# A graph network's edges as two streams on 128 partitions: scans of 64 by 1024 become scans of 128 by 512

## The reference, cut to what matters

```python
def prop(h):                                           # layer 0: Chebyshev, twice
    return segment_sum(w[:, None] * h[src], dst, num_segments=n)
# layer 0 goes on with a softmax over the edges of a node (segment_max, exp, segment_sum), 4 heads,
o = segment_sum(xh[s2] * alpha[:, :, None], d2, num_segments=n)
# layer 1: messages mlp(relu(norm(x[src]))) * et, summed per dst;   layer 2: relu(... @ W + b), summed per dst
# layer 3: hh = [x_dst, x_src - x_dst] @ W.T + b per edge, batch norm over the edges, leaky relu, mean per dst
```

## Time and profile before

| | |
|---|---|
| median of 3 runs | 5640.05 us (5634.35 to 5642.95) |
| span of the profiled execution | 5641.0 us |
| busy: PE, DVE, ACT, POOL | 3732.6, 4168.8, 2361.1, 3788.1 us |

### The profile page before, as it was taken

How to read it: one execution, slowest core, us unless ns; L and a number is a source line. 1 busy time by engine, 2 the same in 40 slices (tenths; PEclk the granted TensorE clock), 3 DMA queues, 4 the chain that set the end, 5 groups by cost and what they waited for, 6 DMA issues and landing times. The chain is left out here.

```text
span 5641.0 us, 69641 instructions
## 1 busy us (share of the span) xinstructions
PE 3732.6 (66%) x15267; PEld 1851.4 (33%) x15267; DVE 4168.8 (74%) x6266; ACT 2361.1 (42%) x4957; POOL 3788.1 (67%) x3734
## 2 busy tenths in 40 slices
PE   8997788847776999677727876777555546552110
PEld 3443555533332333244414442333222212221000
DVE  8876789957774555788868988999655559996442
ACT  0000678833331222466618973343222247772221
POOL 7776766767775777577724337666377767774777
PEclk9998899977876555788869998899766568885555
DMA  5533987744442222455524433333244423332221
GB/s 59 77 53 56 153 203 226 234 136 107 107 106 55 61 63 61 141 182 171 181 64 129 137 117 76 82 83 82 79 130 131 131 69 76 76 73 65 68 72 51
DMA packets 538641, 595.34 MB, mean 106 GB/s; under 512 B 300576, under 2 KB 315046, under 8 KB 536923
## 3 DMA queue, kind: packets, MB, share of 16 engines
q1 hardware_dynamic: 319004, 473.91, 28.7%
q0 software_dynamic: 115712, 91.82, 9.1%
q10 hardware_dynamic: 103840, 28.71, 4.2%
HBM read 354.69 MB, written 303.31 MB: 117 GB/s over the span
## 5 line engine op out<-in xcount | busy, mean ns | idle before, releaser
L1135 POOL DMA_INDIRECT l_got<-d_x,l_near x1176 | 1157.6, 984 | 557.5 <-issue 354.6
L1135 POOL DMA_INDIRECT p_got<-d_h,p_near x392 | 440.2, 1123 | 155.8 <-issue 118.9
L848 PE MATMUL ps<-hot_lo,hot_w 128*128 128x512 bf16 x2352 | 510.0, 380 | 13.4 <-DVE hot_lo L785 13.4
L1135 POOL DMA_INDIRECT p_got<-d_sums,p_near x392 | 401.4, 1024 | 151.7 <-issue 149.3
L2457 POOL DMA_INDIRECT out<-fi_res,fi_near x392 | 381.0, 972 | 181.1 <-issue 118.2
L726 POOL DMA_INDIRECT d_pos<-place,near x392 | 400.2, 1021 | 125.2 <-issue 119.1
L1135 POOL DMA_INDIRECT p_got<-d_ext,p_near x392 | 382.2, 975 | 132.4 <-issue 117.1
L1143 POOL DMA_INDIRECT ln_xd<-d_xt,idsE x304 | 286.9, 944 | 136.8 <-issue 96.9
L2131 PE MATMUL ps<-l_hid,w2n 128*64 128x512 f32 x392 | 234.8, 756 | 162.2 <-DVE l_sums L1308 155.7
L412 PE MATMUL ps<-ident,fi_sums 64*128 64x64 f32 x392 | 53.1, 314 | 424.8 <-DVE fi_sums L1308 424.8
L848 PEld LDWEIGHTS ps<-hot_lo,hot_w 128*128 128x128 bf16 x2352 | 230.6, 98 | 293.2 <-issue 17.3
(11 more groups left out here) (391 smaller groups left out, 10871.3 us busy)
## 6 DMA issues: line engine op xcount, KB each, us to landing
l_xd<-d_x SPq DMA_DIRECT2D x147, 256.0 KB
d_ext<-ln_ext SPq DMA_DIRECT2D x98, 264.0 KB
d_xt<-in_x_wide ACTq DMA_DIRECT2D x49, 520.0 KB
ln_x<-in_x SPq DMA_DIRECT2D x98, 256.0 KB
d_h<-ln_hb SPq DMA_DIRECT2D x98, 256.0 KB, 2.9
d_x<-ln_x SPq DMA_DIRECT2D x98, 256.0 KB
lb_x<-d_x SPq DMA_DIRECT2D x49, 512.0 KB
d_x<-lb_x SPq DMA_DIRECT2D x49, 512.0 KB
```

The costliest lines, as they stand in the source:

```text
L848: last = nc.tensor.matmul(bank(h), hot_w[:, r, k], hot_lo[:, r, 512 * h:512 * h + 512], start=False, stop=False)
L1135: nc.gpsimd.indirect_dma_start(out=out[:, q], out_offset=None, in_=source, in_offset=bass.IndirectOffsetOnAxis(ap=ids[:, q:q + 1], axis=0) ...
```

## The change

The padded edges are cut in the middle into two streams of 25,088 (STREAM). The first runs upward from edge 0; the second is turned round and runs downward from the last edge, so that they meet in the middle. A group is now 512 edges of either stream. In column form that is 128 partitions (64 features of the first stream, 64 of the second) by 512 columns.

- In five phases (attention_sums, gated_messages, relu_messages, edge_convolution, finish_rows) the messages, scans, bias passes and what follows them take 128 by 512. Each pair of products that wrote two halves of 1024 columns on 64 partitions becomes one product with 128 output partitions (`both`), or, where the inputs come as two halves already (`w2n`, `gatw`), as many products as before, with zero blocks in the weights. 8 transposes back become 4 (`transpose_paired`). In edge_convolution 4 products become 2.
- first_propagation and second_propagation keep 65 rows and scan twice 512 columns (`run_both`); what comes behind the scan takes 128 by 512.
- A destination whose edges lie on both sides of the cut: in the last group one product with the matrix `cross` adds the two ends (`meet`), if both ends have the same destination. attention_weights does so twice with `turn`. The matrices are made in degrees (`stream_ends`).
- The batch norm's statistics are kept per stream in 128 partitions and joined by two small products; the load of the last columns (`tail`) goes.
- DRAM tensors in column form have 128 rows of 25,088; transfers of 64 rows by 4 KB become 128 rows by 2 KB, two half stores in attention_sources become one.
- The order of the edges, and so of all gathers and scatters, is the woven one. The gathers and scatters are as many and as large as before.

```diff
+def transpose_paired(nc, out, paired, W):
+    for j in range(S // 2):
+        last = nc.tensor.transpose(out[:, P * j:P * j + P], paired[:, P * j:P * j + P], W.ident[:])
+    return last
+def both(weights):
+    return weights[:].rearrange("p h c -> p (h c)")
...
+def run_both(nc, dve, W, g, par, messages, sums, ends, m):
+    for h in (0, 1):
+        part = slice(HALF * h, HALF * h + HALF)
+        end = HALF * h + HALF - 1
+        last = nc.vector.tensor_tensor_scan(sums[:, par, part], W.same65[:, bass.ds(g * HALF + STREAM * h, HALF)],
+                                            messages[:, part], sums[:, 1 - par, end:end + 1], ALU.mult, ALU.add)
+    if not is_last(g):
+        last.then_inc(m["carry"], 1)
+        return
...
+def run_sums(nc, dve, W, g, par, messages, sums, ends, m):
+    scan = nc.vector.tensor_tensor_scan(sums[:, par], W.same[:, bass.ds(g * HALF, HALF)], messages,
+                                        sums[:, 1 - par, HALF - 1:HALF], ALU.mult, ALU.add)
+    if not is_last(g):
+        scan.then_inc(m["carry"], 1)
+        return
+    scan.then_inc(m["run"], 1)
+    dve.wait_ge(m["met"], 1)
+    nc.vector.tensor_copy(sums[:, par, HALF - 1:HALF], ends).then_inc(m["carry"], 1)
+def meet(nc, pe, W, g, par, sums, ends, m):
+    if is_last(g):
+        hold(pe, m["run"], 1)
+        nc.tensor.matmul(ends, W.cross[:], sums[:, par, HALF - 1:HALF], start=True, stop=True).then_inc(m["met"], 1)
@@ degrees, between the 96th and the 97th tile
+    stream_ends(nc, W, ends, ends_e, part_of, sign_of, done, wait)      # 18 small DVE instructions
...
@@ attention_weights, twice
+    def meet_ends(k, values, combine):
+        done(nc.vector.tensor_copy(met[:, 0:k], values))
+        wait()
+        dve.sem_inc(m["met_ready"], 1)
+        dve.wait_ge(m["met_t"], y[0])
...
@@ attention_sums
-    last = nc.tensor.matmul(bank(4, 2)[0:C, HALF * h:HALF * h + HALF], W.gatw[:, q],
-                            pf[:, h, q], start=q == 0, stop=q == 1)
+    last = nc.tensor.matmul(bank(4), W.gatw[:, q, 1 - h:3 - h].rearrange("p k c -> p (k c)"),
+                            pf[:, h, q], start=h + q == 0, stop=h + q == 2)
...
@@ gated_messages
-    last = nc.tensor.matmul(msg[:, part], W.w2n[:], hid[k][:, part], start=k == 0, stop=k == 1)
+    last = nc.tensor.matmul(msg, W.w2n[:, h], hid[k][:, HALF * h:HALF * h + HALF],
+                            start=h + k == 0, stop=h + k == 2)
...
-    transpose_back(nc, bank(1), sums[:, r % 2], W).then_inc(m["back"], 1)
+    transpose_paired(nc, bank(1), sums[:, r % 2], W).then_inc(m["back"], 1)
@@ relu_messages
-    halves(nc, msg[r % 2], W.l2w, hf[:]).then_inc(m["mm"], 1)
+    nc.tensor.matmul(msg[r % 2], both(W.l2w), hf[:], start=True, stop=True).then_inc(m["mm"], 1)
@@ edge_convolution
-    halves(nc, ended, W.l3ab, df[:, r % 2])
-    halves(nc, bank(4 + 2 * (r % 2), 2)[0:C], W.l3b, hf[:, r % 2]).then_inc(m["mm"], 1)
+    nc.tensor.matmul(ended, both(W.l3ab), df[:, r % 2], start=True, stop=True)
+    nc.tensor.matmul(bank(4 + r % 2), both(W.l3b), hf[:, r % 2], start=True, stop=True).then_inc(m["mm"], 1)
@@ finish_rows
-    sp.dma_start(tail[:], D.hh[:, EDGES - tail_n:EDGES]).then_inc(m["tail"], 16)
...
+    nc.vector.bn_aggr(mv[:], stats[:]).then_inc(m["moments"], 1)
...
+    nc.tensor.matmul(bank(4)[:, 0:2], W.fold_mean[:], mv[:], start=True, stop=True)
+    nc.tensor.matmul(bank(4)[:, 2:3], W.fold_apart[:], mv[:, 0:1], start=True, stop=True).then_inc(m["folded"], 1)
```

More of the change, by code:

```diff
@@ L557, in build @@
         W.floor = sb("floor", [P, 1])
-        phase(degrees, W, D, bank, srcE, dstE, ewE)
-        phase(fold_norms, W, D, bank)
-        phase(lone_nodes, W, D, bank)
-        phase(first_propagation, W, D, bank)
-        phase(second_propagation, W, D, bank)
+        with ExitStack() as early:
+            W.same65 = early.enter_context(nc.sbuf_tensor("same65", [C + 1, EP], U8))
+            phase(degrees, W, D, bank, srcE, dstE, ewE)
+            phase(fold_norms, W, D, bank)
+            phase(lone_nodes, W, D, bank)
+            phase(first_propagation, W, D, bank)
+            phase(second_propagation, W, D, bank)
         with ExitStack() as kept:
@@ L592, in split_rows, with stream_ends @@
             done(nc.vector.tensor_tensor(left, left, back, ALU.subtract))
+def stream_ends(nc, W, ends, end, part_of, sign_of, done, wait):
+    share = (STREAM / EDGES, (EDGES - STREAM) / EDGES)
+    apart = (share[0] * share[1]) ** 0.5
+    sides = ((slice(0, C), slice(C, P)), (slice(C, P), slice(0, C)))
+    done(nc.vector.tensor_tensor(W.flag[:], ends[:, 0:1], ends[:, 1:2], ALU.is_equal))
+    done(nc.vector.tensor_tensor(end[:], W.ident[:, C - 1:C], W.ident[:, P - 1:P], ALU.add))
+    for h in (0, 1):
+        done(nc.vector.memset(part_of[C * h:C * h + C], share[h]))
+        done(nc.vector.memset(sign_of[C * h:C * h + C], apart * (1 - 2 * h)))
+    wait()
+    done(nc.vector.tensor_scalar(W.own_end[:], W.ident[:, P - 1:P], W.flag[:, 0:1], None, ALU.mult))
+    done(nc.vector.tensor_scalar(end[:], end[:], W.flag[:, 0:1], None, ALU.mult))
+    for a, b in sides:
+        done(nc.vector.scalar_tensor_tensor(out=W.cross[:, a], in0=W.ident[:, b], scalar=W.flag[:, 0:1], in1=W.ident[:, a],
+                                            op0=ALU.mult, op1=ALU.add))
+        done(nc.vector.tensor_tensor(W.fold_mean[:, a], W.ident[:, a], W.ident[:, b], ALU.add))
+    wait()
+    done(nc.vector.tensor_scalar(W.own_end[:], W.own_end[:], -1.0, 1.0, ALU.mult, ALU.add))
+    done(nc.vector.tensor_scalar(W.join[:], end[:], -1.0, FAR, ALU.add, ALU.mult))
+    for a, b in sides:
+        done(nc.vector.tensor_scalar(W.turn[:, a], W.ident[:, b], end[:, 0:1], None, ALU.mult))
+    done(nc.vector.tensor_scalar(W.fold_apart[:], W.fold_mean[:], sign_of[:, 0:1], None, ALU.mult))
+    wait()
+    done(nc.vector.tensor_scalar(W.fold_mean[:], W.fold_mean[:], part_of[:, 0:1], None, ALU.mult))
 def load_weights(sp, A, W, parts, loaded):
@@ L651, in degrees @@
         line = t("dst_by_line", [P, 2, CHUNK], I32)
+        ends, ends_e = t("stream_ends", [P, 2], I32), t("stream_end_e", [P, 1])
+        part_of, sign_of = t("part_of", [P, 1]), t("sign_of", [P, 1])
         alike = t("alike", [P, CHUNK], U8)
@@ L1244, in scan @@
                     dve.wait_ge(m["carry"], g + 1)
-                    run_sums(nc, W, g, r % 2, bank(4, 2)[0:C + 1], sums, m)
+                    run_both(nc, dve, W, g, r % 2, bank(4, 2)[0:C + 1], sums, ends, m)
                 ring_loop(dve, GROUPS, [a, messages], [scan])
@@ L1936, in a @@
                     hold(pe, m["al_done"], g)
-                    for n in range(S):
-                        last = nc.tensor.transpose(bank(0)[:, ALPHAS * n:ALPHAS * (n + 1)],
-                                                   alpha[:, r % 2, slot_cols(n)], W.ident[0:ALPHAS, 0:ALPHAS])
+                    for j in range(S // 2):
+                        last = nc.tensor.transpose(bank(0)[:, 2 * ALPHAS * j:2 * ALPHAS * (j + 1)],
+                                                   alpha[:, r % 2, P * j:P * j + P], W.ident[0:2 * ALPHAS, 0:2 * ALPHAS])
                     last.then_inc(m["al_t"], 1)
@@ L2186, in relu_messages @@
         hn = t("l2_hn", [P, S, C])
-        msg, sums = [bank(2 + 2 * k, 2)[0:C] for k in (0, 1)], t("l2_sums", [C, 2, G_ROWS])
+        msg, sums, ends = [bank(2), bank(3)], t("l2_sums", [P, 2, HALF]), bank(5)[:, 0:1]
         hf = t("l2_hf", [P, HALF])
@@ L2282, in b @@
                     act.wait_ge(m["mm"], g + 1)
[L2283 removed]
+                    nc.scalar.activation(msg[r % 2], msg[r % 2], ACT.Relu, bias=col["l2b"]
                                          ).then_inc(m["msg_done"], 1)
@@ L2407, in b @@
                     after(act, m["carry"], g)
-                    nc.scalar.activation(nxt[:, r % 2], W.same[0:C, bass.ds(back(g) * G_ROWS + 1, G_ROWS)], ACT.Copy
+                    nc.scalar.activation(nxt[:, r % 2], W.same[:, bass.ds(back(g) * HALF + 1, HALF)], ACT.Copy
                                          ).then_inc(m["nxt_done"], 1)
```

332 lines of the change are left out of this document (188 added, 144 removed).

## The result

The changed kernel takes 5537.5 us (median of four runs, 5525.5 to 5549.1), the kernel before 5637.8 in the same comparison: ratio 0.982, 95% interval 0.981 to 0.983. It is faster by 1.8%, and 32 us above the forecast of 5505, inside its range. The profiled execution has a span of 5529.8 us, 111 less than before.

| phase | before | after | difference | forecast |
|---|---|---|---|---|
| degrees | 545.0 | 565.1 | +20.1 | +0.5 |
| fold_norms, lone_nodes | 659.2 | 651.0 | -8.2 | 0 |
| first_propagation | 533 | 529 | -4 | -2 |
| second_propagation | 557 | 540 | -17 | -5 |
| attention_sources | 583 | 581 | -1.5 | 0 |

What follows compares the result with a forecast made beforehand. No engine bounds the whole: GpSimd's indirect DMAs pace most gather or scatter phases, DVE gated_messages and attention_sums. Terms -76 - 38 - 12 - 5 - 9 + 0.5 + 3.5 = -136 from 5641.0 give 5505 us, range 5462 to 5562.

Steps and rivals of the forecast that it cites:

- fast kind: gated_messages: groups after a 3.62 us product by w2n, forecast to fall from 12.41 to 10.8 us and become more frequent.
- slow kind's loop: gated_messages, after 5.31 us products: scan, product, transposes, ACT, variances, scan, without the message operation; 12.91 to 11.8 us.
- the slower rival: gated_messages: TensorE's clock falls to 1.2 GHz, loop 14.9 us, +101 us, kernel at 5682; chance 0.02.
- The worry about GpSimd: gated_messages: GpSimd's 10.6 us per group lies near the forecast pace; a denser DVE could lift it to 10.8 or 11.0.
- a sign that the forecast is wrong: The forecast would be wrong if GpSimd's issues grew, scans did not shrink, or gated_messages' PE clock fell under 0.8.
- So the bound passes from DVE to ACT: attention_sums: DVE falls to 6.8 us per group, ACT needs 6.9 to 7.4; 7.15 taken, -38 us.
- The first rival (pace kept): gated_messages and attention_sums keep their pace, -22 and -11 us; kernel at about 5586; chance 0.13.
- ACT's chain: attention_sums: the reason given for pace kept, ACT's chain keeping 7.7 us per group, since ACT waits for PE.
- the 24 small instructions: degrees: 18 of stream_ends and 6 of weights on DVE, 4 us, just covered by its lead; +0.5 us.
- its end of -15: edge_convolution: larger-saving end of the -12 us term for the shorter work behind the last gather; other end -5.
- its end of +6: attention_weights: upper end of the +3.5 us term for two meetings, one more operation and three more stores.

Runs made afterwards that it cites:

- gated_small: The kernel after with the sums and reciprocal deviations of gated_messages' three norms in PSUM bank 5; phase 587.1 us, kernel 5546.6 us (0.984).
- act_wide: The kernel after with ACT's own rows in attention_sums made by 4 instructions of 256 columns instead of 16 of 64; phase 403.9 us.
- late_same: The kernel after with the two half loads of `same` held back until TensorE has finished 240 tiles of degrees; degrees 545.0 us, kernel 5530.6 us (0.980).
- before_more_rows: The kernel before with rows 65 to 127 of `same` loaded as well, read by nothing; degrees 555.5 us.
- att_twice: The kernel after with second_propagation's transposes back and product by att done twice; that phase and attention_sources together 1132 us.

## Why the prediction was right, and where it was not

**gated_messages, right in size, and in mechanism but for one loop.** 11.13 us per group against 11.2, the phase shorter by 76.2 against 76. The scan took 1.28 us, the message 0.75. Behind 18 products by `w2n` of over 5 us the next came 11.4 us later on the mean, behind 30 of 3.67 us it came 10.9 later, where I had 11.8 and 10.8; before, it was 12.8 behind 33 longer ones and 12.3 behind 15 of 3.62. More groups are of the fast kind, as I had expected. But both kinds became 1.4 us shorter, and not 1.10 and 1.63: that the message operation is not in the slow kind's loop was wrong, and that the errors cancel in the mean is luck. The clock was 0.90 over the phase (0.87 before), so the slower rival did not come. The worry about GpSimd was half right: its issue grew from 1.03 to 1.085 us, which I had named as a sign that the forecast is wrong, and gated_small shows that operations with two SBUF inputs do it, but taking that away is worth only some 6 us.

**attention_sums, wrong by 30 us.** The step that failed is "So the bound passes from DVE to ACT". I added up each engine alone and took the largest remainder. But DVE and GpSimd did not run their operations with two SBUF inputs at the same time, and in this phase these follow one another in a row with a sum of its own: 2.28 + 1.75 + 0.69 on DVE and 1.27 + 1.91 on GpSimd are 7.90 us, against a period of 7.93 before and 7.79 after. The rows for it were in the trace of before; I read the sum per engine only. The first rival (pace kept) was right for this phase in its number (-11 against the measured -8), but not in its reason, which was ACT's chain: in act_wide 2 us less of ACT's work changed nothing. The mechanism is shown three ways: 58 us more scans cost 0.6 us, 17 us came back when one of the five operations read PSUM, and the same edit gave nothing that can be told ahead of the change. With 0.69 off, the row is 7.21 us and the period 7.44. The Trainium skill (SBUF — State Buffer, Who interferes with whom) says that a DVE instruction with two SBUF inputs contends with a GpSimd instruction that reads SBUF; the trace agrees, with 1300 against 687 ns. I had used that rule for gated_messages, where it mattered little, and not here.

**degrees, wrong by 20 us, and not in the sum at all.** I weighed the 24 small instructions against TensorE's lead, and that held: TensorE lost 1.5 us from 140 to 150. What I left out is that `same` is loaded twice. GpSimd's 392 scatters are a chain of about 520 us. The last one started 15.3 us ahead of the phase's end before, and with a hole the phase ends 11.7 to 13.6 us behind it, so the chain had only 2 to 4 us of cover. The hole of 26 us moved its last start by 21.9 us, and 20 of these show. It comes in most executions, not in all. Shown is that the second broadcast behind the first makes it (late_same, before_more_rows). Why it falls behind the 113th scatter, and why the same 6.3 MB 50 us later leave none, stays open; the small packets of the index store do not start it.

**The ends, right with one too small.** finish_rows: first scatter 16.7 us into the phase instead of 22.6, -5.9 against -5. edge_convolution -15.4 against -12, just outside its end of -15; its last result begins 25 us behind the last gather's issue instead of 35. relu_messages -2.5 against -2. first_propagation -4 in this execution, but 529 to 539 us over all changed kernels, so nothing that can be told. second_propagation -17 against -5: I had priced the halved passes and the product in the trace's mean durations, but the tail of before ran wholly at a granted clock of 0.50. At that clock the tail became 7.5 us shorter, and in this execution the clock rose in the middle of it and gave 3.6 more. Over the executions of the changed kernels but att_twice, this phase and the next together are 10 to 20 us shorter than before.

**attention_weights, +7.4 against +3.5, outside its end of +6.** The term that was too small is the three more stores. They end the phase, behind everything else: from the first store's issue to the next phase 11.5 us instead of 7.6. These 3.9 us alone are more than the whole term; the two meetings and the added operation make up the rest.

Together: 30 and 20 us too much saved, 4 on attention_weights; 12 on second_propagation, 8 on lone_nodes and about 9 elsewhere the other way, which is the 25 us between 136 and 111. That the median fell into the range owes something to misses of both signs.

## What to carry to other kernels

Where DVE and GpSimd both do elementwise work, add up their operations with two SBUF inputs as if they were one engine's, before asking which engine is full. In this phase a shorter instruction outside that row only moved waits once the row was the longest sum. Reading one operand from a PSUM bank (here one that already held it) takes an operation out of the row. And count every transfer that a new layout adds, a copy of a mask too: a broadcast that nobody waits for can stop the indirect DMAs of a GpSimd chain that has only 2 to 4 us of cover.

## What the runs showed of the hardware

- A DVE addition that starts while GpSimd multiplies from SBUF ends 0.55 us behind it instead of running beside it: 1300 ns median instead of 687. It holds in the other direction: GpSimd's product of 1.91 us took 4.03 when it started 0.02 us behind DVE's. `u`, which reads one SBUF tile and PSUM, ran beside the same product at its usual 0.69 us, and DVE's scan beside GpSimd's sum at its usual 1.27.
- The issue of a gather in gated_messages takes 0.94 us if the norms' operations on DVE read only one SBUF tile, and up to 2.65 us beside three in a row that read two. The Trainium skill (SBUF — State Buffer, Who interferes with whom) infers that a tensor_tensor does not hold up descriptor generation. The issue of an indirect DMA is held up here; whether it is the writing of its descriptors or the reading of its indices, which lie in an SBUF tile (`l_near`), no run tells.
- Two broadcasts of 3.1 MB each, issued within 10 us, stop GpSimd's scatters once, for 18 to 28 us, in eight of the ten executions profiled (a short hole in one, none in another). While such loads run, fewer packets of the scatters go out: 275 in 30 us instead of 611.
- The scan costs 2.33 us for 1024 columns and 1.27 for 512, the first on 64 partitions and the second on 128 (1.26 for 512 columns on 65); a product of fp32 with 128 output partitions takes no longer than one with 64 (0.605 against 0.598 us in attention_sums).
